# Fused expert layer, attention and expert layer on one core: the first tile stream moved to a step's edge, and the first job's order changed

## What is computed

```python
x = x + 0.5 * ffn(layernorm(x))
x = x + attn(layernorm(x))
x = x + 0.5 * ffn(layernorm(x))

# attn: 16 heads of 8 features, per sequence
corr = softmax(einsum('bthd,bThd->bhtT', xc, xc))   # xc: xh less its mean over tokens
out  = einsum('bhtT,bThd->bthd', corr, xh)

# ffn: 8 experts, 128 -> 256 -> 128, the two best by softmax(x @ Wg + bg) are mixed
h = relu(einsum('nd,edh->enh', x, W1) + b1)
y = einsum('enh,ehd->end', h, W2) + b2
out = einsum('end,ne->nd', y, comb)
```

## Time and profile before

| What | us |
|---|---|
| median of 3 runs | 1083.83 (1083.62 to 1083.99) |
| the profiled execution, its own time | 1091.86 |
| its span | 1090.0 |
| TensorE busy | 1039.4 (95%) |
| VectorE busy | 846.4 (78%) |
| ScalarE busy | 825.5 (76%) |
| GpSimd busy | 527.4 (48%) |

### The profile page before, as it was taken

How to read it: one execution, slowest core, us unless ns; L and a number is a source line. 1 busy time by engine, 2 the same in 40 slices (tenths; PEclk the granted TensorE clock), 3 DMA queues, 4 the chain that set the end, 5 groups by cost and what they waited for, 6 DMA issues and landing times.

```text
span 1090.0 us, 20893 instructions
## 1 busy us (share of the span) xinstructions
PE 1039.4 (95%) x6817; PEld 604.7 (55%) x6817; DVE 846.4 (78%) x2314; ACT 825.5 (76%) x1126; POOL 527.4 (48%) x561
## 2 busy tenths in 40 slices
PE   4999999999999999999899999999999999999996
PEld 2787877833323325885232333333268877777785
DVE  6899999966667656775577787777467769999986
ACT  4444544489999998998899999999999964445442
POOL 5454757554344330002556666763300018888883
PEclk9899999999999999999999999999999999999999
DMA  6333222200002412441011111115124613344451
GB/s 194 138 144 117 94 83 95 81 14 20 19 18 64 129 45 68 146 145 70 25 30 38 32 35 38 35 35 173 54 88 136 214 63 103 122 129 152 138 172 37
DMA packets 56830, 96.25 MB, mean 88 GB/s; under 512 B 7819, under 2 KB 28435, under 8 KB 56723
## 3 DMA queue, kind: packets, MB, share of 16 engines
q1 hardware_dynamic: 47298, 76.83, 21.2%
q0 software_dynamic: 8192, 16.79, 5.0%
q10 hardware_dynamic: 1234, 1.29, 0.3%
HBM read 61.60 MB, written 33.29 MB: 87 GB/s over the span
## 4 chain that ended last, share of the span: by engine, by line
PE 65%; ACT 19%; issue 8%; DVE 6%; DMA 1%; SPq 1%; ACTq 0%; POOLq 0%; POOL 0%; DVEq 0%
ACT probs L1782 11%; PE ps L1564 8%; ACT sums L1782 6%; PE ps L636 5%; PE ps L638 5%; PE ps L637 5%; PE ps L652 5%; PE ps L653 5%; PE ps L1549 5%; PE ps L657 5%; PE ps L1204 2%; PE ps L1206 2%; PE ps L1205 2%; PE ps L1215 2%; PE ps L1216 2%
## 5 line engine op out<-in xcount | busy, mean ns | idle before, releaser
L1782 ACT ACTIVATE probs<-ps 128x1024 f32<-128x1024 f32 x344 | 337.2, 1124 | 12.3 <-PE ps L1549 11.3
L1021 ACT ACTIVATE high<-ps 128x512 fp32r<-128x512 f32 x256 | 153.3, 600 | 136.3 <-PE ps L638 125.8
L1505 POOL DMA_INDIRECT found<-tiles,home x128 | 128.2, 1002 | 152.4 <-ACT sums L1782 108.2
L1493 POOL DMA_INDIRECT sorted<-xn,slot x128 | 129.2, 1009 | 142.6 <-ACT probs L1782 90.7
L1092 POOL TENSOR_TENSOR sums<-sums 128x512 f32<-128x512 f32 x111 | 143.7, 1294 | 87.8 <-DVE sums L884 86.7
L1564 PE MATMUL ps<-probs,value 128*32 128x512 f32 x1376 | 184.1, 607 | 1.1 <-issue 0.4
L861 DVE SCALAR_TENSOR_TENSOR low<-ps,high 128x512 fp32r<-128x512 f32 x256 | 163.9, 681 | 14.7 <-ACT high L1021 13.7
L1782 ACT ACTIVATE sums<-ps 128x1024 f32<-128x1024 f32 x168 | 173.1, 1123 | 1.6 <-PE ps L1549 0.9
L1549 PE MATMUL ps<-shared 32*128 32x512 f16 x1024 | 143.0, 385 | 13.5 <-ACT probs L1782 5.7
L1549 PEld LDWEIGHTS ps<-shared 32*128 32x128 f16 x1024 | 38.1, 91 | 144.5 <-ACT probs L1782 64.7
L636 PE MATMUL ps<-xh,weights 128*128 128x512 f32 x256 | 109.5, 428 | 0.0
(11 more groups left out here) (182 smaller groups left out, 1883.3 us busy)
## 6 DMA issues: line engine op xcount, KB each, us to landing
wide<-gates SPq DMA_DIRECT2D x32, 512.0 KB
probs<-gates SPq DMA_DIRECT2D x32, 512.0 KB
found<-sorted SPq DMA_DIRECT2D x46, 256.0 KB, 2.6
tiles<-sums SPq DMA_DIRECT2D x46, 256.0 KB, 2.0
sorted<-zeros SPq DMA_DIRECT2D x16, 512.0 KB
out<-X SPq DMA_DIRECT2D x16, 256.0 KB
X<-in_L_attn_x SPq DMA_DIRECT2D x3, 1024.0 KB, 9.7
sorted<-xn,slot POOLq DMA_INDIRECT x128
```

Of the source, the lines that this page charges most:

```text
L1021: nc.scalar.activation(high[:, third(m), c, :], ps[:, hidden_bank(m, c), :], ACT.Relu).then_inc(sm["f_high"], 1)
L1782: nc.scalar.activation(ring[ring_at(n)], ps[:, score_banks(n), :], ACT.Exp, scale=SCORE).then_inc(sm["a_probs"], 1)
```

## The change

It does the following.

- The pause for the first tile stream moves from group 26 to group 24: from the middle of step 6 to the edge between steps 5 and 6 (`MIDDLE` becomes `TILED`).
- The 8 scatters of job 7 go into the first half of step 5 (as those of job 15 already do in step 15). The 8 gathers of routed sequence 0 are spread over step 6 by `PACE`, followed by two gathers of sequence 1, as later steps have it. Its two combining halves move from the head of step 7 to the last group of step 6. The statistics of routed job 8 go to the second group of step 6, where the other steps have theirs.
- `attn_mix(0, 0)` is issued before `attn_scores(2)` instead of after `attn_scores(4)`.
- For the first tile stream ScalarE copies the rows before it chooses the weights, as it does for the second.
- The lists of the first job change. TensorE: hidden layer 0 right behind the logits. VectorE: job 0's rows ahead of the W1 chunks; the chunks' low halves earlier or later; job 1's statistics and rows ahead of the two halvings. ScalarE and VectorE: the last W1 chunk only behind job 1's rows. GpSimd: W2 chunks 1 to 3 wait until job 1's rows are normalised.

```diff
@@ -48,13 +48,12 @@
 EARLY = 3
 LAST = NJOB - EARLY - 1, 2 * NJOB - 2
 RUSH = NJOB - EARLY, 2 * NJOB - 1
-MIDDLE = WHOLE - 2
-PAUSE = 4 * MIDDLE + 2
+TILED = WHOLE - 2
+PAUSE = 4 * TILED
 
 
 PACE = 2, 4, 7, 8, 10, 12, 13, 16, 17, 20, 22, 24, 26, 27, 30, 32
 LAST_SENDS = 2, 4, 6, 8, 10, 12, 14, 16
-FIRST_COLLECTS = 16, 17, 19, 20, 22, 23, 25, 26
 
 
 RATE = E + 1
@@ -134,7 +133,7 @@
 
 def job_at(s):
 
-    return s + EARLY if 0 <= s < RUSH[0] else s + 1 if MIDDLE < s < RUSH[1] else None
+    return s + EARLY if 0 <= s < RUSH[0] else s + 1 if TILED < s < RUSH[1] else None
 
 
 def early_base(q):
@@ -712,11 +711,10 @@
             if first == 0:
                 ffn_turn(pe, 0)
                 ffn_logits(pe, 0)
+                ffn_hidden(pe, 0)
                 ffn_turn_logits(pe, 0)
                 pe.wait_ge(sm["small_in"], 16 * SMALL)
                 nc.tensor.transpose(ps[:, output_bank(0), 0:E], b2[:, :], ident[0:E, 0:E]).then_inc(sm["b2_turned"], 1)
-            if first == 0:
-                ffn_hidden(pe, 0)
                 ffn_hidden(pe, 1)
                 pe.wait_ge(sm["b2_set"], 1)
                 ffn_turn_gates(pe, 0)
@@ -886,23 +884,22 @@
 
             if first == 0:
                 ffn_stats(dve, 0)
+                ffn_norm_rows(dve, 0)
                 shift_w1(dve, 0)
-                ffn_norm_rows(dve, 0)
+                second_half_of_w1(dve, 0)
+                ffn_low_rows(dve, 0)
                 shift_wg(dve)
-                second_half_of_w1(dve, 0)
                 shift_w1(dve, 1)
-                ffn_low_rows(dve, 0)
                 ffn_ranking(dve, 0)
                 second_half_of_w1(dve, 1)
                 shift_w1(dve, 2)
                 ffn_gating(dve, 0)
+                ffn_stats(dve, 1)
                 halve(0)
+                ffn_norm_rows(dve, 1)
+                halve(1)
                 shift_w1(dve, 3)
-                ffn_stats(dve, 1)
-                halve(1)
                 second_half_of_w1(dve, 2)
-                ffn_norm_rows(dve, 1)
-                second_half_of_w1(dve, 3)
             else:
                 halve(first * E)
                 ffn_low_rows(dve, first + 1)
@@ -917,6 +914,7 @@
                         halve(m + 2)
                     if m == 0:
                         ffn_low_rows(dve, 1)
+                        second_half_of_w1(dve, 3)
                     if m == 1:
                         scale(0)
                         ffn_ranking(dve, 1)
@@ -1036,7 +1034,6 @@
                 relu(1)
                 first_half_of_w2(act, 1)
                 ffn_copy_gates(act, 0)
-                first_half_of_w1(act, 3)
                 first_half_of_w2(act, 2)
                 first_half_of_w2(act, 3)
             else:
@@ -1054,6 +1051,7 @@
                     if m == 0:
                         ffn_copy_rows(act, 1)
                         ffn_copy_high(act, 1)
+                        first_half_of_w1(act, 3)
                     if m == 1:
                         ffn_copy_logits(act, 1)
                         ffn_copy_turned(act, 1)
@@ -1096,6 +1094,7 @@
                 ffn_ties(pool, 0)
                 second_half_of_w2(pool, 0)
                 norm_pool(pool, "f_", 1, side(1))
+                pool.wait_ge(sm["f_xn"], 2)
                 for q in range(1, CHUNKS):
                     second_half_of_w2(pool, q)
             ffn_ties(pool, first + 1)
@@ -1464,12 +1463,9 @@
                                      bias=b2T[:, bass.ds(of[t], 1)]).then_inc(sm["t_y"], 1)
 
             for i in stream(a, b):
-                if i == a - 2 and a == 0:
-                    choose(a)
-                    choose(a + 1)
                 if in_stream(i + 2, a, b):
                     x_high(i + 2)
-                if i == a - 2 and a > 0:
+                if i == a - 2:
                     choose(a)
                     choose(a + 1)
                 if in_stream(i + 1, a, b):
@@ -1582,9 +1578,11 @@
                 job, earlier = job_at(s), job_at(s - 1)
                 for k in range(UNITS):
                     n = g * UNITS + k
+                    if n == 0:
+                        attn_mix(pe, 0, 0)
                     if n + 2 < b * UNITS:
                         attn_scores(pe, n + 2)
-                    if k % 2 == 0 and n >= a * UNITS + 2:
+                    if k % 2 == 0 and n >= max(a * UNITS + 2, 4):
                         attn_mix(pe, (n - 2) // UNITS, (n - 2) % UNITS // 2)
 
                     if n == 2:
@@ -1735,9 +1733,6 @@
                 if hg == 0 and s in RUSH:
                     group_counts(dve, RUSH.index(s))
                 if hg == 0 and more:
-                    if s + 1 == WHOLE:
-                        combine_half(dve, 0, 0)
-                        combine_half(dve, 0, 1)
                     if WHOLE <= s + 1:
                         dve.wait_ge(sm["c_added"], s + 2 - WHOLE)
                     if s > 0:
@@ -1760,11 +1755,11 @@
                     group_tiles(dve, RUSH.index(s))
                 if hg == 1 and earlier is not None:
                     route_gates(dve, earlier)
-                if hg == (2 if s == MIDDLE else 1) and job_at(s + 1) is not None:
+                if hg == 1 and job_at(s + 1) is not None:
                     route_stats(dve, job_at(s + 1))
                 if hg == 3 and job is not None:
                     route_rank(dve, job)
-                if hg == 3 and WHOLE < s + 2 < S:
+                if hg == 3 and WHOLE <= s + 2 < S:
                     combine_half(dve, s + 2 - WHOLE, 0)
                     combine_half(dve, s + 2 - WHOLE, 1)
 
@@ -1829,23 +1824,20 @@
                     attn_values(pool, s + 1)
                 if i == 14 and job_at(s + 1) is not None:
                     norm_pool(pool, "r_", job_at(s + 1), job_at(s + 1) % 2)
-                if s == RUSH[1]:
+                if s in RUSH:
                     if half == 0:
                         pool.wait_ge(sm["a_probs"], first + LAST_SENDS[i])
                         send(pool, earlier, i)
                 elif earlier is not None and i % 2 == 0:
                     pool.wait_ge(sm["a_probs"], first + PACE[i])
                     send(pool, earlier, i // 2)
-                if q == 0 and half == 1:
-                    pool.wait_ge(sm["a_probs"], first + FIRST_COLLECTS[i - 8])
-                    collect(pool, 0, i - 8)
-                if q == 1 and i in (0, 1, 2, 3, 5, 7, 9, 11):
+                if q == 0 and i in (0, 1, 2, 3, 5, 7, 9, 11):
                     pool.wait_ge(sm["a_probs"], first + PACE[i])
-                    collect(pool, 1, i if i < 4 else i // 2 + 2)
-                if 1 < q < NJOB and i % 2 == 1 and i < 12:
+                    collect(pool, 0, i if i < 4 else i // 2 + 2)
+                if 0 < q < NJOB and i % 2 == 1 and i < 12:
                     pool.wait_ge(sm["a_probs"], first + PACE[i])
                     collect(pool, q, i // 2 + 2)
-                if 0 < q < NJOB - 1 and i in (13, 15):
+                if 0 <= q < NJOB - 1 and i in (13, 15):
                     pool.wait_ge(sm["a_probs"], first + PACE[i])
                     collect(pool, q + 1, i // 2 - 6)
 
```

## The result

The changed kernel took 1081.97 us (median of 10 runs, 1079.95 to 1083.44), the kernel before 1084.51 on the same chip (10 runs, 1083.62 to 1086.50). The ratio of the times is 0.9972, its 95% interval 0.9962 to 0.9982: 0.28% faster. Forecast were 5.1 us and 1078.7; the time lies inside the range of 1075.2 to 1083.0, but above the forecast's own, 1076.5 to 1080.5. The profiled execution of the changed kernel took 1080.28 us, with a span of 1078.4.

What follows compares the result with a forecast made beforehand. The prediction took a relay as the bound, its last-ending chain 65% TensorE and 19% ScalarE. Its terms, -2.3 + 0.7 - 1.7 - 1.8 = -5.1 us, carried to the plain median of 1083.83, gave 1078.7, range 1075.2 to 1083.0.

Steps and rivals of the forecast that it cites:

- (b): First job: the start gives nothing, GpSimd's subtractions blocking other VectorE instructions and late gates eating the rest; 1081.0, chance 0.22.
- (d): Tiles: their part gives nothing, step 6 keeps its losses and the entry only moves the wait; 1082.2, chance 0.10.
- The start: First job: faster normalisation of job 1's rows, less late gates and blocked instructions, saves 2.3 us.
- The ranking: First job: hidden layer 0 ahead of the logits' turn makes the gates and all behind them 0.8 us later.
- The two blocked instructions: First job: GpSimd's subtractions block a W1 shift and a W1 second half on VectorE, 0.6 us each.
- The mixing: Start of attention: the mixing finds no hole and pushes back scores and exponentials, costing 0.7 us.
- The entry: First tiles: copying rows before weights brings the first hidden matmul closer to the last exponential, saving 1.7 us.
- Steps 5 to 7: Around the first tiles: step 6 in one piece and no combining in step 7's head save 1.8 us.
- The doubt: Behind the tiles: such pauses may belong to the profiled execution alone, so part of the savings was not counted.
- the two savings: Step 6 shorter by 1.0 us and step 7 by 1.65, counted as 0.6 and 1.2.
- (c): Start and tiles: TensorE keeps the full clock through the start, both pauses behind the tiles go; 1075.5, chance 0.14.
- Rival (e): Job 0: spread pauses put four more experts at TensorE's low clock, +11.6 us, making it slower; 1090.3, chance 0.04.

Runs made afterwards that it cites:

- start only: The kernel before with only the first job's lists of the change, GpSimd's wait included; 1093.81 us, ratio 0.9988.
- Wait only: The kernel before with one line added: GpSimd waits for job 1's normalised rows; 1091.50 us, ratio 0.9967.
- mixing only: The kernel before with only the first mixing moved ahead of the scores of unit 2; 1086.36 us, ratio 1.0014.
- before again: The kernel before, without any edit, run and profiled once more on a slower chip; 1094.70 us, ratio 0.9999.
- tiles only: The kernel before with only the tiles at the step's edge and the scatters, gathers, combining and statistics that go with it; 1089.99 us, ratio 0.9960.
- the same, old entry: The kernel before with GpSimd's wait and the tiles at the step's edge, weights still copied ahead of the rows; 1080.36 us, ratio 0.9952.
- mixing back: The changed kernel with the first mixing back at its old place, behind the scores of unit 4; 1087.56 us, ratio 0.9938.
- after again: The changed kernel, without any edit, run once more on one of the slower chips; 1088.36 us, ratio 0.9940.
- halving first: The changed kernel with the first mixing at its old place and hidden 0 halved ahead of job 1's statistics; 1089.36 us, ratio 0.9945.
- no wait: The changed kernel without GpSimd's wait for job 1's rows; 1083.62 us, ratio 0.9990.
- entry only: The kernel before with only the rows copied ahead of the weights at the first tiles' entry; 1094.30 us, ratio 0.9992.
- wait, tiles, entry: The kernel before with GpSimd's wait, the tiles at the step's edge and the rows ahead of the weights; 1077.95 us, ratio 0.9939.

## Why the prediction was right or wrong

**The number and the mechanism.** The measured time lies where rivals (b), 1081.0, and (d), 1082.2, put it, above the forecast's own range. The experiments bear out the forecast's mechanisms all the same, term by term; what took the rest is below, under the sum.

**The start, -2.3, came to -2.43**, and its terms held. The normalisations were forecast at 1.11 and took 1.11. The ranking was to start 0.8 later and started 0.89 later (15.75 against 14.86). The two blocked instructions were priced at 0.6 each and cost 0.12 and 1.09 (0.80 and 1.77 where 0.68 is usual). The Trainium skill, "SBUF — State Buffer", the section on the shared port, would have allowed 2 x 1.32; only one of the two came near. The first scaling was forecast near 32.7 and came at 32.56, and job 1's ranking no longer waits. One reading was wrong and cost nothing: VectorE did have a pause in this stretch of the kernel before, 0.53 at 30.72. The mechanism of rival (b) is refuted: "start only" has its first exponential 2.56 earlier. But in the plain runs that kernel gained only 0.12% (0.03 to 0.21%), so a part of (b)'s outcome, a start that brings little at the end, did come; its profile puts that down to low stretches elsewhere and not to blocked instructions. What I missed is that two of these terms, together 2.1, are costs of the new lists that bring nothing back. "Wait only" has neither, its gates stay early, TensorE has one pause of 1.9 instead of 3.45 and 1.08, and the low clock doesn't come.

**The mixing, +0.7, came to +0.97.** The step was right. The term was sized too low: the mixing's whole 1.07 is paid, less 0.1, and I had put 0.9 as its upper end.

**The entry, -1.7.** The first hidden matmul came 1.73 earlier, as forecast. The gap between the two exponentials' starts shrank by 1.35 (1.12 alone), since 0.54 is given back inside the tiles; the last exponential itself is 0.14 shorter. I read the second stream's entry only up to its first matmul, and took that for the end of the matter.

**Steps 5 to 7, -1.8.** The mechanism was right: one piece instead of two, and the combining out of step 7's head. The size depends on the chip: -1.68 where the chip has no pauses of its own (89.02 in "mixing only" against 87.34), -2.88 where it has ("before again" against "tiles only"). Where the low clock also falls behind the tiles, the old form takes 91.55 to 91.79, some 1.1 more again; this happened in four of the six profiles of the old form and in none of the new. The doubt that pauses behind the tiles belong to the profiled execution alone was half right: on the chip of "mixing only" steps 8 to 13 have none, while on the slower chips the plain runs are as long as the profiled one (medians near 1095), which speaks for their having them too. Discounting the two savings for that doubt, to 1.8 from 2.65, brought the forecast near the 1.68.

**The sum.** On the first chip the terms measured make -2.43 + 0.97 - 1.35 - 1.68 = -4.5, close to the -5.1 forecast. The plain runs gave -3.0. They fall in two groups. Four of the ten, the profiled one among them, took 1079.95 to 1080.76, with the clock at 0.995 or 0.996 over the span. Six took 1081.80 to 1083.44 at 0.993. The first group is about 4.0 below the kernel before, the second about 2. So what the sum lacked is a term for the low stretches, whose number varies between executions of one kernel. The same split stands in "the same, old entry" (1078.6 and 1080.5) and in "mixing back" (1087.4 and 1089.0). Whether the start's form makes it more frequent isn't shown: on the second kind of chip the same kernel ("after again") had no run at 0.993. Where the six lose their 2 us no profile of them shows; a second low stretch in the first job, as "halving first" has at 34 to 39, or one in the tiles would fit, and this stays open. Carrying the sum of one execution to the median was the weak point. That the time still fell inside the range owes something to the range's width, which was made for (c) and (d).

**Rival (e)**, the low clock in job 0, didn't decide, but it named the right place. It came in "halving first" and "no wait", each with a second low stretch in job 0. I gave it a price of several experts, 11.6, where one such stretch costs 1.6 to 1.9 (gaps 90.03 and 91.66; the two groups of "the same, old entry"): the changed kernel couldn't become slower by it.

**Rival (d)** was refuted by "tiles only" (-2.88 in steps 5 to 7) and "entry only" (gap 1.12 less), (c) by the low clock that stayed in 22.7 to 26.1. The profile of "wait, tiles, entry" comes nearest to what (c) describes: the start 4.8 shorter than before and no low stretch.

## What to carry to other kernels

When a change holds one engine back to keep a shared resource free for another, try that wait alone before the lists around it are rewritten: here one line brought the first exponential forward by 5.1, and with the new order only 2.5 of that was left. Judge a pause of TensorE not only by its length but by the clock behind it, and take the piece that removes the pause (rows ahead of weights) before the piece that only moves it. A saving found at one place is to be followed to the end of the span: in the profile of "start only", 2.56 us won at the start were 0.94 at the end of the tiles. And a saving read from one profile is the saving of one execution: look at how the plain runs spread, and at their clock, before it is carried to the median.

## What was not expected of the hardware

- The chips differ. The kernel before took 1084.5 in two blocks of the table and 1095 in the two others (whether the first and the last block were on one chip isn't known). Of the 10.5 us between them 7.6 lie in steps 8 to 13 (185.8 against 178.2), in every kernel of a block alike; the first profile of the kernel before, with 182.66, lies between. There ScalarE waits up to 0.4 at a time for scores, at the full clock. What delays them was not found.
- The same pause at the entry of the tiles, 2.11 us in the same code, was followed by the full clock in three profiles (gaps 90.03 to 90.12) and by a low stretch in four others, whose code differs only elsewhere and which come to it at another time (gaps 91.56 to 91.66). Each is one execution, and of "the same, old entry" two runs of five have too high a clock (0.998) for such a stretch. So whether the shift in time decides, or chance, isn't shown; what is shown is that this stretch costs 1.6 us at a place that a change such as "mixing only" doesn't touch.
